# A decoder layer on one core: context sums added ahead of the cross products, context pieces rounded later, last base pieces made behind the first turned tokens

## What is computed

```python
def _L0_attn_ref(x, w_qkv, b_qkv, w_o, b_o):
    qkv = x @ w_qkv.T + b_qkv
    ...
    scores = jnp.where(causal[None, None, :, :], scores, jnp.float32(-1e+20))
    attn = jax.nn.softmax(scores, axis=-1)
    ...
    return out @ w_o.T + b_o
def _L0_xattn_ref(x1, x2, x1_scale, x1_zp, x2_scale, x2_zp):
    ...
        q = jnp.clip(jnp.round(x / s + z), QMIN, QMAX)
        return (q - z) * s
    ...
    return jnp.matmul(q1, q2)
def _L0_ffn_ref(x, W_org, lora_down, lora_up, lora_keys, Wq):
    base = jnp.einsum('bsi,oi->bso', x, W_org)
    q = jnp.einsum('bi,ki->bk', x.mean(axis=1), Wq)
    scores = jnp.einsum('bk,ek->be', q, lora_keys) / math.sqrt(K)
    coeffs = jax.nn.softmax(scores, axis=-1)
    h = jnp.einsum('bsi,eir->bser', x, lora_down)
    delta = jnp.einsum('be,bser,ero->bso', coeffs, h, lora_up)
    return base + delta * (SCALE * MULTIPLIER)
```

## Time and profile before

| what | us |
|---|---|
| median of 3 runs (712.63 to 716.53) | 715.35 |
| the profiled execution's own time | 713.16 |
| its span, first to last instruction | 711.2 |
| TensorE busy | 654.7 (92%) |
| VectorE busy | 427.1 (60%) |
| ScalarE busy | 423.6 (60%) |
| POOL busy | 284.5 (40%) |
| mean granted TensorE clock | 0.980 |

### The profile page before, as it was taken

One profiled execution on the slowest core, in us unless ns is written; L12 is line 12 of the kernel. 1 busy time (PEld: TensorE's weight loads), 2 busy tenths in 40 slices (PEclk: granted clock), 3 DMA queues, 4 the chain that ended last, 5 costly groups with the idle time before them and its releaser, 6 DMA issues.

```text
span 711.2 us, 12688 instructions
## 1 busy us (share of the span) xinstructions
PE 654.7 (92%) x4512; PEld 531.0 (75%) x4512; DVE 427.1 (60%) x1135; ACT 423.6 (60%) x1025; POOL 284.5 (40%) x309
## 2 busy tenths in 40 slices
PE   4997899999999899999888699999999889799998
PEld 3985677898777678787656577787878667688886
DVE  6795677875867634666776965442226789811122
ACT  5425678878878748689967675755315683520320
POOL 2047645524444344455320730505715016813520
PEclk9999999999999989999999899999999999999999
DMA  8658754742555723325552350404327263613102
GB/s 267 227 150 236 242 130 126 223 135 75 145 161 160 218 64 98 104 57 139 178 183 73 96 135 1 148 1 151 127 80 236 79 195 98 196 52 108 45 18 100
DMA packets 43933, 93.46 MB, mean 131 GB/s; under 512 B 5504, under 2 KB 5888, under 8 KB 42432
## 3 DMA queue, kind: packets, MB, share of 16 engines
q1 hardware_dynamic: 34416, 66.45, 29.3%
q0 software_dynamic: 3696, 15.73, 9.3%
q10 hardware_dynamic: 5760, 10.49, 4.0%
HBM read 72.72 MB, written 19.92 MB: 130 GB/s over the span
## 4 chain that ended last, share of the span: by engine, by line
PE 64%; DVE 15%; ACT 10%; issue 5%; POOL 4%; DMA 2%; ACTq 0%; DVEq 0%
PE dense L1067 32%; PE probt L955 8%; PE score L1067 7%; PE pv L971 5%; PE score L943 5%; PE pv L1067 3%; DVE stats L1363 3%; POOL w_lo L1686 2%; ACT prob_all L1161 2%; DVE xres L1467 2%; ACT w_hi L1114 1%; PE misc L980 1%; DVE prob_all L1319 1%; DVE prob_all L1444 1%; ACT stage L1110 1%
## 5 line engine op out<-in xcount | busy, mean ns | idle before, releaser
L1319 DVE CUSTOM_DVE_ANT_0 prob_all<-score,mask_sb 128x128 f32<-128x128 f32 (+3 forms) x256 | 123.1, 487 | 115.6 <-PE score L943 113.9
L1686 POOL TENSOR_TENSOR w_lo<-stage,w_hi 128x512 fp32r<-128x512 f32 x85 | 110.0, 1302 | 199.7 <-ACT w_hi L1114 199.4
L1067 PE MATMUL dense<-w_hi,act_t 128*128 128x512 f32 (+1 forms) x536 | 181.2, 392 | 5.8 <-POOL act_t L1697 1.9
L1161 ACT ACTIVATE prob_all<-prob_all,neg_max 128x128 f32<-128x128 f32 (+3 forms) x256 | 142.8, 558 | 40.0 <-DVE neg_max L1319 38.6
L1067 PE MATMUL dense<-act_t,w_hi 128*128 128x512 f32 x366 | 124.9, 423 | 1.3 <-POOL w_lo L1686 1.2
L955 PE MATMUL probt<-ident_sb,prob_all 128*128 128x128 f32 x640 | 114.2, 278 | 5.8 <-ACT prob_all L1170 3.6
L1067 PEld LDWEIGHTS dense<-w_hi,act_t 128*128 128x128 f32 x536 | 101.1, 195 | 22.8 <-issue 3.9
L1067 PE MATMUL dense<-w_lo,act_t 128*128 128x512 f32 (+1 forms) x298 | 107.6, 379 | 1.4 <-ACT w_lo L1119 1.1
L955 PEld LDWEIGHTS probt<-ident_sb,prob_all 128*128 128x128 f32 x640 | 80.2, 143 | 24.1 <-issue 8.4
L1114 ACT ACTIVATE w_hi<-stage 128x512 fp32r<-128x512 f32 x117 | 72.0, 622 | 42.6 <-PE dense L1067 18.4
L1170 ACT ACTIVATE prob_all<-probt 128x128 f32<-128x128 f32 (+3 forms) x160 | 68.5, 428 | 48.2 <-PE probt L955 46.9
(11 more groups left out here) (204 smaller groups left out, 1014.6 us busy)
## 6 DMA issues: line engine op xcount, KB each, us to landing
q_stack<-rope_dram POOLq DMA_DIRECT2D x15, 768.0 KB, 7.1
stage<-in_w_qk SPq DMA_DIRECT2D x40, 256.0 KB, 2.9
rope_dram<-act_t ACTq DMA_DIRECT2D x40, 256.0 KB, 2.8
stage<-in_w_o SPq DMA_DIRECT2D x32, 256.0 KB, 3.0
stage<-in_ctx_kv SPq DMA_DIRECT2D x24, 256.0 KB, 3.3
stage<-in_w_org SPq DMA_DIRECT2D x24, 256.0 KB, 3.1
xres<-in_x SPq DMA_DIRECT2D x8, 512.0 KB, 6.3
prob_all<-in_x SPq DMA_DIRECT2D x8, 512.0 KB, 6.8
```

Source lines behind the costliest of these rows:

```text
L1067: last = engine.matmul(dst, lhs, rhs, start=(k == 0 and c == 0), stop=(k == g.kts - 1 and c == len(pairs) - 1))
L1161: engine.activation(prob[:, u % P_SLOTS, 0:length], prob[:, u % P_SLOTS, 0:length], ACT.Exp, bias=neg_max[:, m:m + 1], scale=-1.0, accum_o ...
L1319: engine.tensor_tensor_reduce(prob[:, u % P_SLOTS, 0:length], score_bank[u % 2][:, 0:length], mask_sb[:, S - length:S], -1.0, HIGHEST, ALU ...
L1686: engine.tensor_tensor(slot_lo(p, 0, NW), raw_of(p), slot_hi(p, 0, NW).bitcast(F32), ALU.subtract).then_inc(g_piece, 1)
```

## The change

Three rules of the plan change, with the waits that they need.

1. A context piece's rounding is no longer noted in the slot of its dequantising: it is queued, and noted at the first slot that lies at least one later and, behind the attention stage, 1.5 us later by the plan's clock (`ROUND_US`). The centring follows it as before.
2. A correction no longer waits for the cross tile to be added. It is placed once the context sum is out and the row's correction known (`CORRECT_US` after the third step of the quantised tokens), one per slot at most in the attention stage. Where it comes first, it waits for the output tile's addition, and L1489 waits for it. The statistics of the last norm and the base tile's addition wait for both.
3. Pieces 144 to 151 (the base pieces of batch 1's left half) are not made high or low before the tokens of tile 0 of batch 1's last norm are turned; pieces behind them in the queue follow. And the chain of tile 3 of that norm moves from VectorE to POOL.

```diff
-CHAINS_ON_VECTOR = [(which, b, t) for which, b in ((1, 0), (1, 1), (2, 1)) for t in range(NT)] + [(3, 1, 3)]
+CHAINS_ON_VECTOR = [(which, b, t) for which, b in ((1, 0), (1, 1), (2, 1)) for t in range(NT)]
...
+            if self.behind_tokens(p, 0) and ("tokens", 3, 1, 0, 1) not in self.done:
+                break
             self.note("hi", j, p)
             if cross:
-                self.note("round", j + 1 if unit else j, p)
+                self.to_round.append(p)
...
+        while self.to_round:
+            p = self.to_round[0]
+            if not self.past(j, ("hi", p), 1, now, 0.0 if unit else ROUND_US):
+                break
+            self.note("round", j, p)
+            self.to_round.pop(0)
...
+    def behind_tokens(self, p, ahead):
+
+        piece = self.pieces[p]
+        return (piece["kind"], piece["b"], piece["nb"]) == ("base", 1, 0) and piece["k"] >= ahead
...
-                if ("correct",) + what in self.done or not self.past(j, ("evac", "cross", b, nb, n), 0):
+                if ("correct",) + what in self.done or corrected and unit:
                     continue
-                if self.past(j, ("context", b, nb), 0):
+                if self.past(j, ("context", b, nb), 0) and self.past(j, ("third", b, n), 2, now, CORRECT_US):
                     self.note("correct", j, what)
                     self.correct_order.append((b, nb, n))
-                    if ("correct", b, n, 1 - nb) in self.done:
-                        self.norms.append({"no": (3, b, n), "from": j})
+                    corrected = True
...
-                e.wait_ge(*evacuated("cross", b, nb, t))
+                e.wait_ge(*evacuated("out" if corrected_first(b, nb, t) else "cross", b, nb, t))
...
                     e.wait_ge(*evacuated("out", g.b, g.nb, n))
+                    if corrected_first(g.b, g.nb, n):
+                        e.wait_ge(*corrected(g.b, g.nb, n))
...
                         e.wait_ge(*corrected(g.b, g.nb, n))
+                        e.wait_ge(*evacuated("cross", g.b, g.nb, n))
```

## The result

| what | before | changed |
|---|---|---|
| median, us (4 runs each, on one chip) | 713.99 (711.87 to 716.53) | 702.5 (701.59 to 703.62) |
| ratio, 95% interval | | 0.9843, 0.982 to 0.9866 |
| profiled execution's own time | 713.16 | 701.59 |
| its span | 711.2 | 699.8 |
| mean granted TensorE clock | 0.980 | 0.985 |

The change is faster (1.6%, the interval leaves out 1), as forecast, but by 11.5 us where 7.8 were forecast. The median of the kernel before is 1.4 us lower here (four runs) than the 715.35 from which the forecast was taken (three).

What follows compares the result with a forecast made beforehand. TensorE is busy 92%, so only its holes and lower-clock time (12.75 us) can be won. Terms 4.9 + 2.6 + 0.9 = 8.4, less 0.6, leave 7.8 us: 707.5 against the median 715.35, range 703.0 to 712.8 us.

Steps and rivals of the forecast that it cites:

- Term 1: 549 to 582 us: with rounding later, VectorE stops waiting for ScalarE and TensorE turns quantised tile 3 4.9 us earlier.
- Term 2: Last norm, up to the first base product: early corrections, four POOL chains and later base pieces win 2.6 us.
- hand-overs: VectorE's gaps of 0.2 to 0.4 us between instructions, not all placed in the schedule: 0.6 us taken off the gain.
- Term 3: Batch 0, attention stage: moved corrections win 0.9 us, bounded by 0.7 dearer and 1.6 cheaper.
- The clock: Last norm, behind TensorE's shortened wait: granted clock full instead of 0.52, where the half clock had cost 1.6 us.
- B: Corrections of the second half stay dear beside POOL, 1.5 us instead of 0.67: gain 4.5, 710.9 us; chance 0.13.
- C: Waits move to the first context sum, clock may fall again: gain 0 to 3, 712.5 to 715.4 us; chance 0.16.
- D: TensorE starves at the first base product as POOL's low parts come late: slower, 719.8 us; chance 0.05.
- E: VectorE was idle where the wait goes and ScalarE paces the tiles, so less gain; chance counted in C.

Runs made afterwards that it cites:

- round_alone: Kernel before with only the later rounding; corrections, base pieces and last chain as before: ratio 0.9921, 707.34 us.
- base_alone: Kernel before with only the base pieces behind the turned tokens and the last chain on POOL: ratio 0.9968, 711.64 us.
- no_corr: Changed kernel with the corrections back behind their cross tiles, rounding and base pieces as changed: ratio 0.9885, 706.14 us.
- b0_alone: Kernel before with only batch 0's corrections (attention stage) placed early, everything else as before: ratio 1.0003, 713.57 us.
- corr_alone: Kernel before with only the corrections placed ahead of the cross products: ratio 0.9983, 712.15 us.
- beside_sbuf: Changed kernel plus five VectorE additions with two SBUF inputs behind batch 1's last five cross tiles, result unread: ratio 0.9869, 705.12 us.
- beside_psum: Changed kernel plus the same kind of five unread VectorE additions, first input from a PSUM bank instead of SBUF: ratio 0.9853, 703.99 us.
- no_round: Changed kernel with the roundings back in the slot of their dequantising, corrections and base pieces as changed: ratio 0.9936, 708.63 us.

## Why the prediction was right in kind and short in size

**Term 1, the rounding: right.** From the first quantised turning to that of tile 3 it took 25.85 us (556.04 to 581.89) and takes 21.10 (553.57 to 574.67): 4.75 us, forecast 4.9. The prediction named what would be late next, the context sum, and gave it 1.2 us; it waits 1.01.

**Term 2, the last norm: mis-sized, 2.6 forecast, 4.2 measured.** The stretch as a whole gives 8.9 us, less 4.75. The statistics of tile 0 came as forecast (585.63, or 588.1 when the profiles are laid on each other at the first quantised turning, 2.47 us apart; forecast 587.7). The step that failed is the price of a chain on POOL: "Three chains took POOL from 594.72 to 605.10, 3.46 us each ... Now POOL does four, 13.8 us". In those three, corrections of VectorE held four instructions for 0.4 to 0.5 us each (two of them in the third chain); the change moves these corrections away, so the four take 11.5 us, 2.3 less. TensorE's path has three of them. The third ended at 595.91, or 598.4 laid on the old profile, where 599.6 was forecast, and everything behind it came as much earlier: the tokens of tile 1 freed at 604.6 and 605.8 (forecast 606 to 607.1), the first base product at 609.9 (forecast 611.3). The forecast waits of TensorE there were 1.8 + 2.5 + 0.1 = 4.4 us; they are 0.35 + 0.48 + 0.83 + 0.47 = 2.1. Its own work took 15.2 us where the forecast has 14.5, partly since two turnings are done in halves, so that 1.6 us of the 2.3 are left. The 0.6 us taken off for hand-overs had nothing to stand for either: the bare schedule of term 1 held to 0.15 us.

**Term 3, batch 0: 0.9 forecast, nothing measured in the total** within 1.4 us. The wait that the prediction named is 1 us shorter (2.57 to 1.53), so the cheaper side was seen rightly; the value between the two bounds was not worth its decimal.

**The rest, 2.1 us, stays open.** The stretch explains 8.9 of 11.0 us. The difference lies ahead of 554 us, in the profiles too (2.47 us at the first quantised turning), but 1.35 of it is there at TensorE's first small turning of the attention stage (101.84 before, 100.49 changed), where both kernels have run the same instructions, and that mark lies between 100.44 and 104.75 in the profiles of kernels that are equal up to there. The corrections of batch 0 are not the cause, and the later roundings of batch 0 hardly: `round_alone`, with these roundings, gained as much by its ratio (5.6 us) as its stretch shows. The table has a hint that I hadn't followed. Gain by ratio less gain of the stretch is -0.1 to 1.0 us in the four altered kernels with batch 1's corrections late (`round_alone`, `base_alone`, `no_corr`, `b0_alone`), and 0.9 to 4.8, on average 2.5, in the fifteen rows with them early; one such value is uncertain by 1.3 to 2.4 us. So the rest seems to go with this part of the change, although it lies ahead of all the instructions that the part moves: up to 540 us `b0_alone` (-0.1) and `corr_alone` (3.2) run the same work in the same order on VectorE, ScalarE and POOL. What carries it, the program's layout or something else, no run shows.

**What put the time outside the range.** From 7.8 to 11.0 us: term 1 took 0.15 away, term 2 added 1.6, term 3 took 0.9, the hand-overs added 0.6, the open rest added 2.1. That the third and fourth of these nearly cancel is luck. The stretch alone, 8.9 us, lies within the forecast's own 5.5 to 10.5; with the rest the gain doesn't. The absolute time also had the 1.4 us in it by which the median of the kernel before was lower than the one forecast from.

**The clock: right here, by a wrong reading.** With no wait over 1.01 us behind 554 us the granted clock is 1.00 where it was 0.52, and the first wait of the last norm costs no second time. That was 1.6 us of the holes and losses that the prediction listed. But its ground, that "no other hole of this trace under 3.1 us was followed by a lower clock", doesn't hold in that trace. Behind the 2.57 us of the earlier trace rows stands another wait of the kernel before, with the clock of the window after it:

```profile
406.06 1.11 PE L924 MATMUL misc<-ident_sb,xnorm 128*128 128x128 f32 x4 [2.40 <-DVE tok_sum L1418]
```

```profile
404.00:410.00 6.00, 3.94 (x13) 0.50 0.38 112
```

Four such transposes take 0.63 us at the full clock, 8 us earlier. With the 1.8 and 2.5 us of waiting that the prediction forecast for the last norm, it had no ground to put the clock at full there; the waits came out short enough.

**The rivals.** B (corrections stay dear beside POOL) didn't come: POOL's subtractions end at 581.58, and the four corrections, started at 581.47, take 0.67 us each, as the prediction argued. The Trainium skill's rule (SBUF — State Buffer, "SBUF: two separate sides") held all the same, but on the side that I hadn't priced: by `beside_sbuf` and `beside_psum` it is POOL that was held by the corrections, so the rule spoke for the change and not against it. C (waits move on to the context sum, clock falls) didn't come in the whole change, though its clock did in `corr_alone` and `no_round`. D (TensorE starves) was far: POOL starts the low parts at 598.78, and the first is wanted at 607.42. E: the waits of VectorE went, as the change says. After the first base product no low part was waited for (86.58 us busy of 86.58).

**The range** took its low end from the forecast "below the fastest of the runs shown", not from a case in which term 2 is larger, and no sum gives the 703.0: 10.5 us below the median is 704.9, and below the fastest run 702.1. The prediction had 3.46 us as the only price of a chain, and the only other chain in its rows is VectorE's, 2.2 us; the bound from below should have been four chains at the sum of their instructions' normal lengths. For the three chains on TensorE's path, 0.55 us each, that would have given up to 1.7 us more, 705.8 at the centre and about 701.3 at the end.

## What to carry to other kernels

Before a duration from the old profile is laid on the new order, look at what ran beside it, and whether the change moves that away. Here one long instruction in a chain of eight short ones gave it away. Parts of a change that each shorten the same chain are worth more together than alone, if a hole that one leaves open is taxed a second time by the clock: measure them by leaving them out as well as alone. And the stage that a change moves, timed within one profile, is steadier than the total by a factor of ten or more.

## What the runs showed of the hardware

- A VectorE instruction of 128x512 with two SBUF inputs (0.74 us) holds a POOL instruction of 128x1 that meets it: 0.65 to 0.74 us instead of 0.19 to 0.34 (`beside_sbuf`; 0.59 to 0.86 in the kernel before). With one input from PSUM it doesn't (`beside_psum`).
- The other way round, roundings and centrings of VectorE, one SBUF input and 128x512, took 1.35 and 1.52 us beside POOL's subtractions (576.39 and 577.66, POOL busy from 576.15 to 581.58) where they take 0.42 alone; the additions of cross tiles from PSUM right behind them, beside the same subtractions, took their usual 0.70 (1.40 for two at 579.10). The Trainium skill's section named above gives both forms: two SBUF inputs, and a VectorE operation in a mode that takes both ports; these two rows agree with the second.
- How long TensorE had waited before a turning of the last norm, and the time of the eight transposes then (1.03 to 1.09 at the full clock, 2.22 at half): 4.46, 4.07, 3.50 and 2.87 us were followed by 2.21 to 2.22; 2.65, 2.56 and 2.15 by a normal first half and a slow second (1.07 to 1.11 for four, normally 0.66); 1.91 and less by nothing. At the quantised turnings a wait of 3.05 left the clock at 1.00, and one of 2.21, 17.6 us behind such a wait, was followed by 0.50 (`corr_alone`, `no_round`). In the attention stage of the kernel before, 2.57 and 2.40 us close to each other were followed by 0.50. So the length of one wait doesn't decide it alone.
